# A decoder layer on one core: splitting the weights and forming the merged query weights inside the first sequence's work

## The chip, the core and the metric

The kernel runs on one core of a Trainium2 chip. The core has five engines that run their own instruction streams in order: PE (TensorE, matmuls, with its weight loads shown as PEld), DVE (VectorE), ACT (ScalarE), POOL (GpSimd) and SP (SyncE, which here only issues DMAs). They are tied together by semaphores alone. The metric is the device time of one execution in microseconds (us).

## What is computed

One pre-norm decoder layer on x of 2 x 1024 tokens with 512 channels: a windowed self-attention, a cross-attention to a context of 2 x 2048 tokens, and a feed-forward part. The reference, cut to what matters here:

```python
qkv = _layernorm(x) @ qkv_w.T + qkv_b            # 16 heads of 32; q and k scaled to length 1
attn = softmax(where(abs(i - j) <= 16 and (i - j) % 2 == 0, q @ k.T, -inf))
x = x + (attn @ v) @ out_w.T + out_b
q = _layernorm(x) @ Wq + bq
k, v = ctx @ Wk + bk, ctx @ Wv + bv
x = x + softmax(q @ k.T) @ v
x = x + (silu(x_n @ w_gate.T) * (x_n @ w_up.T)) @ w_down.T     # x_n = _layernorm(x), weights int / 127
```

The kernel never forms the cross-attention's keys. It multiplies the normalised x by one merged matrix, the product of Wq and Wk (`wp`), and the context itself is then the key. The biases go into a column `bqp`, a scalar `bqbk` and a row `wqb_row`; the value bias of the first attention goes through the output weights into `ob_row`.

## The kernel before

Every float32 matmul that matters is done as three matmuls on a high and a low part of each operand (`three`, L164 to L168: high x high, high x low, low x high). So each weight is split once: ACT casts the raw weight to the high part (`wqkv_h`), DVE subtracts it from the raw weight to get the low part (`wqkv_l`).

There are two blocks of engine programs in `attention_phase`. **The setup block** (L282 to L391) runs first and alone: SP loads all weights, POOL writes the constants (`ident`, `band`, `ones`, `hmask`, `mhalf`), ACT and DVE split Wq, Wk, the output weights and the first attention's weights `wqkv`, PE forms the bias rows and columns and the product `wp` in the four `score` banks, and ACT and DVE split that product. It ends with DVE copying the bias results. All engines meet at its end.

**The main block** (from L452) then goes through NS = 4 sequences `s` of 512 tokens in tiles of 128 tokens (ST = 4). For a sequence: DVE takes mean and variance of a tile (`spread1`), POOL the root (`root1`), ACT normalises (`norm1`), PE transposes (`transposes`), ACT and DVE split the result (`turned`), PE projects to queries and keys (`project_qk`) and to values (`project_v`). `p` is 0 or 1 for the first or second half of the head groups, and the columns of `wqkv` for p = 1 are not read before the loop. DVE copies q and k out with their bias (`qk_tile`), ACT squares, DVE sums (`square_sums`) and from the sums of four tiles finds 1 / length in a chain of 14 small instructions (`lengths`, L832 to L854), POOL scales q and k by it (`scale_units`, 128x1024 each), PE transposes them (`heads`, 8 transposes for a group), ACT and DVE split those (`heads_hi`, `heads_lo`). After that lead-in of sequence 0 a loop runs over `s` and n = 0 to 15, a unit being one of 4 head groups in one of 4 token tiles: `scores` on PE, `exp` on ACT, `mask` on POOL, `weighted` on PE. In each unit PE also does a piece of the next sequence's projections, or of the previous sequence's output and query projections. The later stages (cross-attention, feed-forward) follow.

The order on each engine is written out by hand in the code. PE's results other than scores go through `work`, a ring of four PSUM banks whose uses are listed in `ring_uses`; PE takes the n-th use only when the (n-4)-th has been read out (`take`, `wait_freed`). The use `("len", ...)` is one in which DVE computes the lengths inside the bank, so the fourth value tile of sequence 0 waits for the end of `lengths`. SP issues its DMAs in the order of its program, and waits in it hold back all that stands behind.

## Time and profile before

| what | value |
|---|---|
| median of 3 runs | 1280.5 us (1279.76 to 1282.55) |
| the profiled execution, its own time | 1279.2 us |
| its span in the profile | 1277.5 us |
| PE busy / DVE / ACT / POOL | 95% / 43% / 32% / 19% |
| setup block, up to the first instruction of the main block | 39.6 us |
| lead-in of sequence 0, up to the first projection of the loop | 39.6 to 75.0 us |

The span is what the trace covers; 1.7 us of the profiled execution lie around it. A busy share is taken over the whole span. PE's is high everywhere but at the start, so what is read for this change is the first 146 us, stretch by stretch. In a timeline row stand the start, the duration or the length of a merged stretch (x2, x16: so many instructions), the engine, the line, the operation with output and inputs, and in brackets the idle time before it and what ended that.

### The profile page before, as it was taken

Reading aid. Unit: us, or ns where it says so; the run is one execution under the profiler, and the core shown is the slowest. Engines: PE = TensorE matmul, PEld = TensorE weight load, DVE = VectorE, ACT = ScalarE, POOL = GpSimd, SP = SyncE. Lnnn points to the kernel's source line nnn. Section 1 sums busy time; section 2 is a strip of 40 time slices with the busy share of each in tenths; the row PEclk is TensorE's granted clock in tenths of the full one; section 3 lists DMA queues with packets and bytes.
Section 4 is the critical chain, followed back from the end, with each engine's and each line's share of the span. In section 5 each row is a group of like instructions: output and inputs, shape, how many; then the busy total and the mean of one; then the engine's idle time right before and its main releaser. Section 6 shows DMA issues by size and latency. Waiting matters only on the chain.

```text
span 1277.5 us, 16905 instructions
## 1 busy us (share of the span) xinstructions
PE 1219.5 (95%) x6760; PEld 984.0 (77%) x6760; DVE 553.8 (43%) x1030; ACT 414.7 (32%) x740; POOL 239.3 (19%) x230
## 2 busy tenths in 40 slices
PE   6889999999987989999999999999999999999998
PEld 4667777777755878888787888877888888888887
DVE  5446666585675643223554322334353123123212
ACT  4235454445353432322442222223332111111111
POOL 0136665655664110000000000000000000000000
PEclk9789999999979999999999999999999999999999
DMA  6200020200044341010250110043321001000000
GB/s 247 66 8 27 2 66 2 75 34 34 34 149 149 124 148 42 26 33 25 99 173 22 37 32 26 17 140 96 100 62 67 1 1 48 18 0 24 9 1 33
DMA packets 45763, 73.29 MB, mean 57 GB/s; under 512 B 4225, under 2 KB 16513, under 8 KB 45697
## 3 DMA queue, kind: packets, MB, share of 16 engines
q1 hardware_dynamic: 45696, 72.37, 17.3%
q8 instruction: 46, 0.75, 0.3%
q14 instruction: 21, 0.16, 0.0%
HBM read 55.58 MB, written 16.78 MB: 57 GB/s over the span
## 4 chain that ended last, share of the span: by engine, by line
PE 78%; DVE 6%; issue 5%; ACT 3%; POOL 3%; DMA 1%; DVEq 0%; POOLq 0%; ACTq 0%
PE work L166 13%; PE work L168 12%; PE work L167 12%; PE score L166 11%; PE score L168 11%; PE score L167 11%; PE score L1054 2%; PE work L1559 2%; DVE rsum L871 1%; PE score L1068 1%; PE work L1037 1%; PE work L1013 1%; POOL xs L556 1%; DVE ct_l L1439 1%; PE score L1072 1%
## 5 line engine op out<-in xcount | busy, mean ns | idle before, releaser
L166 PE MATMUL score<-fxt_h,w_hl 128*128 128x512 f32 x384 | 149.6, 390 | 0.8 <-DVE fxt_l L1822 0.8
L168 PE MATMUL score<-fxt_h,w_hl 128*128 128x512 f32 x384 | 149.4, 389 | 0.0
L167 PE MATMUL score<-fxt_l,w_hl 128*128 128x512 f32 x384 | 149.4, 389 | 0.0
L1842 DVE SCALAR_TENSOR_TENSOR hid<-score,gate 128x512 f32<-128x512 f32 x48 | 33.2, 691 | 236.6 <-ACT gate L1771 236.6
L1445 DVE TENSOR_TENSOR pt_l<-work,pt_h 128x512 fp32r<-128x512 f32 x64 | 44.0, 690 | 181.3 <-ACT pt_h L1372 181.3
L1771 ACT ACTIVATE gate<-score 128x512 f32<-128x512 f32 x48 | 28.7, 598 | 265.9 <-PE score L168 265.9
L166 PE MATMUL score<-ct_h,x_q_h 128*128 128x512 f32 x256 | 103.5, 404 | 3.9 <-DVE x_q_l L1434 3.2
L537 POOL TENSOR_TENSOR probs<-probs,band 128x544 f32<-128x544 f32 (+1 forms) x64 | 91.1, 1424 | 73.2 <-ACT probs L658 72.9
L166 PE MATMUL work<-cn,pt_h 128*128 128x512 f32 x256 | 101.6, 397 | 0.0
L168 PE MATMUL score<-ct_h,x_q_l 128*128 128x512 f32 x256 | 100.7, 393 | 0.0
L167 PE MATMUL score<-ct_l,x_q_h 128*128 128x512 f32 x256 | 100.2, 391 | 0.0
L168 PE MATMUL work<-cn,pt_l 128*128 128x512 f32 x256 | 99.9, 390 | 0.0
L167 PE MATMUL work<-cn,pt_h 128*128 128x512 f32 x256 | 99.7, 390 | 0.0
L166 PE MATMUL work<-wqkv_h,xt_h 128*128 128x512 f32 (+1 forms) x256 | 93.9, 367 | 2.3 <-DVE rnrm L854 1.9
L1372 ACT CAST pt_h<-work 128x512 fp32r<-128x512 f32 x64 | 37.2, 587 | 178.2 <-PE work L1559 178.2
L1351 POOL TENSOR_TENSOR xr<-xr,bv_row 128x512 f32<-128x512 f32 x16 | 21.5, 1342 | 392.3 <-DMA xr<-x_scratch 392.3
L168 PE MATMUL work<-wqkv_h,xt_l 128*128 128x512 f32 (+1 forms) x256 | 87.6, 342 | 0.0
L167 PE MATMUL work<-wqkv_l,xt_h 128*128 128x512 f32 (+1 forms) x256 | 87.5, 342 | 0.0
L166 PEld LDWEIGHTS score<-fxt_h,w_hl 128*128 128x128 f32 x384 | 72.1, 188 | 16.2 <-issue 1.2
L168 PEld LDWEIGHTS score<-fxt_h,w_hl 128*128 128x128 f32 x384 | 72.1, 188 | 15.1
L167 PEld LDWEIGHTS score<-fxt_l,w_hl 128*128 128x128 f32 x384 | 72.1, 188 | 14.8
L166 PE MATMUL work<-w_hl,hid_h 128*128 128x512 f32 x192 | 75.5, 393 | 0.9 <-DVE xr L1475 0.8
(180 smaller groups left out, 2474.3 us busy)
## 6 DMA issues: line engine op xcount, KB each, us to landing
x_stage<-in_ctx_t SPq DMA_DIRECT2D x16, 512.0 KB, 4.0
x_stage<-in_ctx_n SPq DMA_DIRECT2D x16, 512.0 KB, 4.1
x_in<-in_x SPq DMA_DIRECT2D x16, 256.0 KB, 2.7
xs<-in_x SPq DMA_DIRECT2D x4, 1024.0 KB, 5.4
x_scratch<-xs SPq DMA_DIRECT2D x4, 1024.0 KB, 4.4
qp_scratch<-xs SPq DMA_DIRECT2D x4, 1024.0 KB, 4.3
x_q_raw<-qp_scratch SPq DMA_DIRECT2D x16, 256.0 KB, 2.7
xr<-x_scratch SPq DMA_DIRECT2D x16, 256.0 KB, 2.7
```

Source lines behind the costliest of these rows:

```text
L166: pe.matmul(out, hi_s, hi_m, start=first, stop=False)
L167: pe.matmul(out, hi_s, lo_m, start=False, stop=False)
L168: return pe.matmul(out, lo_s, hi_m, start=False, stop=last)
L537: PL.tensor_tensor(probs[:, n % 2, :, 0:w], probs[:, n % 2, :, 0:w], band[:, c0:c0 + w].unsqueeze(1).to_broadcast([P, HPG, w]), ALU.mult). ...
L556: PL.tensor_tensor(xs[:, t, :], xs[:, t, :], ob_row[:], ALU.add).then_inc(xb_done, 1)
L1054: last = PE.matmul(out[a], kt[r, g % 2, c], qt[r, g % 2, :, lo:lo + w], start=first_mm, stop=last_mm)
L1351: nc.gpsimd.tensor_tensor(xr[:, par, :], xr[:, par, :], bv_row[:], ALU.add).then_inc(xb_done, 1)
L1372: nc.scalar.copy(pt_h[:, 4 * c:4 * c + 4, :], src.rearrange("p (k q) -> p k q", q=P)).then_inc(pth_done, 1)
L1445: V.tensor_tensor(pt_l[:, 4 * c:4 * c + 4, :], src.rearrange("p (k q) -> p k q", q=P), pt_h[:, 4 * c:4 * c + 4, :].bitcast(F32), ALU.subtr ...
L1559: last = PE.transpose(out[:, P * k:P * k + P], pr[:, 512 * c + P * k:512 * c + P * k + P], ident[:])
L1771: nc.scalar.activation(gate[:, f % 2, :], score[:, 2 * (f % 2), :], ACT.Silu, scale=WSCALE)\
L1842: V.scalar_tensor_tensor(hid[:], score[:, 2 * (f % 2) + 1, :], WSCALE, gate[:, f % 2, :], ALU.mult, ALU.mult).then_inc(hid_done, 1)
```

## The change

The setup block is gone. Its work stands in the programs of the main block, in the order of first use:

- SP issues the first three x tiles first, then the first half (p = 0) of `wqkv` in four pieces, then (after a wait on the first normalised tile, in `next_tile(3)`) a fourth x tile, the bias columns, Wq, Wk, the second half of `wqkv` in four pieces, and the output weights. The load of `xs` moves to the loop, behind the split of the output weights, whose raw copy now lies in the same memory.
- A list `parts` names all splits in order: four of p = 0 (128x768 each), `wide` (the key bias spread over 128 columns), Wq, Wk, four of p = 1, the second `wide`, the output weights. `part_hi(n)` is the cast on ACT, `part_lo(n)` the subtraction on DVE.
- PE: the bias row `wqb` (now 12 matmuls in split form, before 4 plain float32 ones) stands before the first value tile; `product(0)` and `product(1)` around the fourth value tile, `product(2)` and `product(3)` behind `heads`; the bias columns (20 matmuls of one column) behind the first `scores`; the row `ob` (12 matmuls) in unit n = 14 of sequence 0. The four uses `wqb`, `bq`, `bk` and `ob` go through the ring, which DVE empties.
- In the loop of sequence 0, ACT and DVE do one 128x512 split at n = 0 and the 128x2048 split of the output weights at n = 12.
- POOL writes the constants at the start of its main program.

```diff
+            if not s and n == 14:
+                yield ("ob",)
...
+            for t in range(3):
+                sp.dma_start(x_in[:, t, :], x_v[0][:, t, :]).then_inc(xin_landed[t], 16)
+            for k in range(DK):
+                sp.dma_start(raw[:, 0, k, :], wqkv_v[:, 0, k, :]).then_inc(wqkv_landed[0][k], 16)
...
+            def part_hi(n):
+                src, hi, _, landed, count = parts[n]
+                act.wait_ge(landed, count)
+                A.copy(hi, src).then_inc(set_hi, 1)
...
+            part_hi(KEYS)
+            part_hi(WQ)
             squares(0, 0, 2)
+            part_hi(WK)
             squares(0, 0, 3)
-            for t in range(ST):
+            for k in range(DK):
+                part_hi(SECOND + k)
+            for t in range(3):
                 v_tile(0, 0, t)
+            product_hi(0)
+            v_tile(0, 0, 3)
+            product_hi(1)
+            act.wait_ge(consts, CONSTS)
+            act.wait_ge(set_lo, VALUES)
             heads_hi(0, 0)
...
+                    if not s and n in (0, 12):
+                        part_hi(WO if n else VALUES)
...
+            def part_lo(n):
+                src, hi, lo, _, _ = parts[n]
+                dve.wait_ge(set_hi, n + 1)
+                V.tensor_tensor(lo, src, hi.bitcast(F32), ALU.subtract).then_inc(set_lo, 1)
...
             transposes("x", 0, 0)
             transposes("x", 0, 1)
+            pe.wait_ge(set_lo, DK)
             project_qk(0, 0, 0)
...
             project_qk(0, 0, 3)
+            pe.wait_ge(set_lo, WQ + 1)
+            bias_row(("wqb",), 0, q_h, q_l)
             leave(("len", 0, 0))
-            for t in range(ST):
+            for t in range(3):
                 project_v(0, 0, t)
+            pe.wait_ge(set_lo, WK + 1)
+            product(0)
+            project_v(0, 0, 3)
+            product(1)
             heads(0, 0)
             heads(0, 1)
+            product(2)
+            product(3)
+            pe.wait_ge(prod_lo, 2)
             scores(0, 0)
+            bias_columns()
+            pe.wait_ge(prod_lo, DK)
...
+                    if not s and n == 14:
+                        pe.wait_ge(set_lo, WO + 1)
+                        bias_row(("ob",), 1, wo_h, wo_l)
```

**DVE, lead-in of sequence 0**, from the second tile's sum of squares on. Before:

```order
L823 TENSOR_REDUCE ss<-sq 128x16
L817 TENSOR_TENSOR qk<-work,qkb_row 128x2x256
L823 TENSOR_REDUCE ss<-sq 128x16
L817 TENSOR_TENSOR qk<-work,qkb_row 128x2x256
L823 TENSOR_REDUCE ss<-sq 128x16
L832 TENSOR_SCALAR work<-ss 128x64
```

Between the sums of the second tile and the first instruction of `lengths` (L832) stand only the two remaining tiles. The same place after the change (line numbers of the changed kernel):

```order
L816 TENSOR_REDUCE ss<-sq 128x16
L902 COPY wide<-cols 128x1024
L805 TENSOR_TENSOR wide_l<-wide,wide_h 128x512
L805 TENSOR_TENSOR wq_l<-wq_raw,wq_h 128x2048
L810 TENSOR_TENSOR qk<-work,qkb_row 128x2x256
L816 TENSOR_REDUCE ss<-sq 128x16
L805 TENSOR_TENSOR wk_l<-wk_raw,wk_h 128x2048
L810 TENSOR_TENSOR qk<-work,qkb_row 128x2x256
L816 TENSOR_REDUCE ss<-sq 128x16
L911 COPY wqb_row<-work 128x512
L825 TENSOR_SCALAR work<-ss 128x64
```

Three subtractions and two copies have moved in ahead of `lengths`; four more subtractions (128x768) follow directly behind it.

**PE, from the last `heads` of the lead-in to the first projection of the loop.** Before:

```order
L1037 MATMUL work<-ident,qk 128x128 x16
L1054 MATMUL score<-qbd_h,kt_h 128x2x136 x2
L1054 MATMUL score<-qbd_l,kt_h 128x2x136 x2
L1054 MATMUL score<-qbd_h,kt_l 128x2x136 x2
L1054 MATMUL score<-qbd_h,kt_h 128x288 x2
L1054 MATMUL score<-qbd_l,kt_h 128x288 x2
L1054 MATMUL score<-qbd_h,kt_l 128x288 x2
L166 MATMUL work<-wqkv_h,xt_h 128x512
```

After, from the last three of the 24 matmuls of `product(2)` and `product(3)`, which stand behind the 16 transposes:

```order
L168 MATMUL score<-wk_h,wq_h 128x512
L169 MATMUL score<-wk_l,wq_h 128x512
L170 MATMUL score<-wk_h,wq_l 128x512
L1108 MATMUL score<-qbd_h,kt_h 128x2x136 x2
L1108 MATMUL score<-qbd_l,kt_h 128x2x136 x2
L1108 MATMUL score<-qbd_h,kt_l 128x2x136 x2
L1077 MATMUL work<-cols,wk_raw 128x1 x16
L1082 MATMUL work<-cols,wide 128x1 x4
L1108 MATMUL score<-qbd_h,kt_h 128x288 x2
L1108 MATMUL score<-qbd_l,kt_h 128x288 x2
L1108 MATMUL score<-qbd_h,kt_l 128x288 x2
L168 MATMUL work<-wqkv_h,xt_h 128x512
```

The products stand between the transposes and the first `scores`, the 20 one-column matmuls between the first and the second.

**DVE in units n = 12 to 14 of sequence 0**, from the end of `lengths` for sequence 1 on, after the change:

```order
L847 RECIPROCAL rnrm<-work 128x4x2x8
L864 RECIPROCAL rsum<-rsum 128x256
L805 TENSOR_TENSOR wo_l<-wo_raw,wo_h 128x2048
L864 RECIPROCAL rsum<-rsum 128x256
L853 TENSOR_TENSOR kt_l<-work,kt_h 128x512
L857 SCALAR_TENSOR_TENSOR qbd_l<-work,hmask,qbd_h 128x512 x2
L983 TENSOR_TENSOR ob_row<-work,ob_row 128x512
```

`wo_l` has come between the two halves of the softmax sum's reciprocal (`rsum`), which before followed each other at once; POOL's `out_scale`, and behind it `mask` and `scale_units`, wait for the second half.

## Rows read from the trace of the kernel before

**Rows 1.** The page: chain that ended last, and DMA issues (median us to landing).

```profile
PE 78%; DVE 6%; issue 5%; ACT 3%; POOL 3%; DMA 1%; DVEq 0%; POOLq 0%; ACTq 0%
...
x_in<-in_x SPq DMA_DIRECT2D x16, 256.0 KB, 2.7
```

**Rows 2.** Windows: stretch, length, busy by engine, PE clock, DMA share, GB/s.

```profile
0.00:39.60 39.60, 26.82 (x104) 17.98 (x104) 17.88 (x16) 14.63 (x12) 1.92 (x16) 0.96 0.56 199
39.60:74.97 35.37, 27.71 (x140) 22.77 (x140) 19.44 (x52) 13.30 (x23) 7.92 (x11) 0.80 0.19 60
...
146.00:1277.50 1131.50, 1097.48 (x5890) 891.42 (x5888) 473.14 (x875) 350.89 (x640) 187.20 (x168) 0.99 0.17 55
...
15.00:20.00 5.00, 5.00 (x17) 3.09 (x16) 2.55 (x2) 0.00 (x0) 0.00 (x0) 1.00 1.01 413
```

**Rows 3.** Timeline, the first weight cast, and the start of the main block.

```profile
6.10 1.90 ACT L331 CAST wq_h<-wq_raw 128x2048 fp32r<-128x2048 f32 x1 [4.01 <-DMA wq_raw<-in_wq_t]
...
39.63 0.69 DVE L790 BATCH_NORM_STATS2 stats<-x_in 128x6 f32<-128x512 f32 x1
...
41.80 0.81 ACT L609 ACTIVATE xn<-x_in,nb,rstd 128x512 f32<-128x512 f32 x1 [12.95 <-POOL nb L514]
...
45.18 0.80 PE L166 MATMUL work<-wqkv_h,xt_h 128*128 128x512 f32 x1 [0.39 <-DVE xt_l L811]
```

**Rows 4.** Timeline, from the last projection of the lead-in to the loop's first.

```profile
59.38 0.39 PE L168 MATMUL work<-wqkv_h,xt_l 128*128 128x512 f32 x1
...
61.99 0.23 DVE L832 TENSOR_SCALAR work<-ss 128x64 int32<-128x64 int32 x1
...
65.99 0.39 PE L166 MATMUL work<-wqkv_h,xt_h 128*128 128x256 f32 x1 [1.91 <-DVE rnrm L854]
66.02 3.79 POOL L531 TENSOR_TENSOR qk<-qk,rnrm 128x1024 f32<-128x1024 f32 x2 [18.21 <-DVE rnrm L854]
...
67.99 3.46 PE L1037 MATMUL work<-ident,qk 128*128 128x128 f32 x16 [0.27 <-POOL qk L531]
...
74.98 0.80 PE L166 MATMUL work<-wqkv_h,xt_h 128*128 128x512 f32 x1
```

**Rows 5.** Groups by line of the setup: busy us, mean ns | idle before.

```profile
L351 DVE TENSOR_TENSOR wqkv_l<-w_raw,wqkv_h 128x1536 fp32r<-128x1536 f32 x4 | 6.8, 1752 | 4.4 <-ACT wqkv_h L336 4.4
...
L348 DVE TENSOR_TENSOR wq_l<-wq_raw,wq_h 128x2048 fp32r<-128x2048 f32 x1 | 2.3, 2287 | 0.0
...
L344 DVE COPY wide<-cols 128x1024 f32<-128x1024 f32 x1 | 0.7, 695 | 10.3 <-DMA cols<-in_qkv_b 10.3
...
L336 ACT CAST wqkv_h<-w_raw 128x1536 fp32r<-128x1536 f32 x4 | 5.6, 1476 | 5.6 <-DMA w_raw<-in_wqkv_t 5.6
```

**Rows 6.** Timeline of PE in the setup: products, one-column matmuls, output bias row.

```profile
16.77 0.79 PE L166 MATMUL score<-wk_h,wq_h 128*128 128x512 f32 x1
...
28.06 0.95 PE L381 MATMUL work<-cols,wide 128*128 128x1 f32 x8
...
32.44 4.52 PE L389 MATMUL work<-wo_raw,wide 128*128 128x512 f32 x6
```

**Rows 7.** Windows in which PE's granted clock (third value from the end) is halved.

```profile
33.40:36.60 3.20, 3.20 (x5) 1.32 (x4) 0.00 (x0) 0.00 (x0) 0.00 (x0) 0.50 0.00 0
67.76:70.95 3.19, 2.96 (x13) 2.66 (x14) 0.69 (x1) 1.91 (x4) 2.05 (x2) 0.50 0.02 5
```

**Rows 8.** Timeline of units n = 12 to 14 of sequence 0.

```profile
129.26 0.65 ACT L658 ACTIVATE probs<-score 128x576 f32<-128x576 f32 x1 [0.83 <-PE score L1054]
...
133.40 1.09 PE L1037 MATMUL work<-ident,qk 128*128 128x128 f32 x8 [1.36 <-POOL qk L531]
...
139.20 1.09 PE L1037 MATMUL work<-ident,qk 128*128 128x128 f32 x8 [0.46 <-POOL qk L531]
```

**Rows 9.** Timeline of sequence 1, unit n = 8: POOL and DVE side by side.

```profile
192.37 1.43 POOL L537 TENSOR_TENSOR probs<-probs,band 128x576 f32<-128x576 f32 x1
192.61 1.74 DVE L884 SCALAR_TENSOR_TENSOR xn<-xn,wqb_row 128x512 f32<-128x512 f32 x1
```

More of the change, by code:

```diff
@@ L258, in attention_phase @@
     x_v = x.rearrange("(s t p) d -> s p t d", t=ST, p=P)
[L260 to L263 removed]
+    raw = over.put("w_raw", [P, 2, DK, PW])
+    raw_o = over_xs.put("wo_raw", [P, DK, D])
+    raw_q = over_wo.put("wq_raw", [P, DK, D])
+    raw_k = over_wo.put("wk_raw", [P, DK, D])
     q_h = over_ot.put("wq_h", [P, DK, D], F32R)
     q_l = over_ot.put("wq_l", [P, DK, D], F32R)
[L266 to L267 removed]
+    wide = over_sums.put("wide", [P, 2, DK, P])
+    wide_at = over_x2t.at
     k_h = over_x2t.put("wk_h", [P, DK, D], F32R)
     k_l = over_x2t.put("wk_l", [P, DK, D], F32R)
[L270 to L271 removed]
+    over_k = Plan(nc, wide_at)
+    wide_h = [over_rows.put("wide0_h", [P, DK, P], F32R)]
+    wide_l = [over_rows.put("wide0_l", [P, DK, P], F32R)]
+    wide_h.append(over_k.put("wide1_h", [P, DK, P], F32R))
+    wide_l.append(over_k.put("wide1_l", [P, DK, P], F32R))
+    wqkv_landed = [[sem(f"wqkv_landed{p}{k}") for k in range(DK)] for p in range(2)]
+    w_landed = [sem(f"w_landed{n}") for n in "qko"]
+    cols_landed = sem("cols_landed")
+    qkb_landed = sem("qkb_landed")
+    ob_landed = sem("ob_landed")
     set_hi = sem("set_hi")
@@ new lines, in attention_phase @@
+    wqkv_v = wqkv_t.rearrange("(k p) (g n) -> p g k n", p=P, g=2)
+    pieces_of = [[(raw[:, p, k, :], wqkv_h[:, k, p, :], wqkv_l[:, k, p, :], wqkv_landed[p][k], 16)
+                  for k in range(DK)] for p in range(2)]
+    bias_of = [(wide[:, n], wide_h[n][:], wide_l[n][:], wide_ready, 1) for n in range(2)]
+    parts = pieces_of[0] + [bias_of[0], (raw_q[:], q_h[:], q_l[:], w_landed[0], 16),
+                            (raw_k[:], k_h[:], k_l[:], w_landed[1], 16)]
+    parts += pieces_of[1] + [bias_of[1], (raw_o[:], wo_h[:], wo_l[:], w_landed[2], 16)]
@@ L473, in _ @@
                     next_tile(k)
+                if not s:
+                    sp.wait_ge(set_lo, WO + 1)
+                    sp.dma_start(xs[:], x_v[0]).then_inc(xs_landed, 16)
                 if s:
@@ L903, in _ @@
             square_sums(0, 0, 1)
+            dve.wait_ge(cols_landed, 64)
+            V.tensor_copy(wide[:], cols[:, 1:3, :].unsqueeze(3).to_broadcast([P, 2, DK, P])).then_inc(wide_ready, 1)
+            part_lo(KEYS)
+            part_lo(WQ)
             qk_tile(0, 0, 2)
             square_sums(0, 0, 2)
+            part_lo(WK)
             qk_tile(0, 0, 3)
             square_sums(0, 0, 3)
+            wait_filled(dve, ("wqb",))
+            V.tensor_copy(wqb_row[:], bank(("wqb",))).then_inc(dve_freed, 1)
             lengths(0, 0)
+            for k in range(DK):
+                part_lo(SECOND + k)
+            product_lo(0)
+            product_lo(1)
+            dve.wait_ge(consts, CONSTS)
             heads_lo(0, 0)
+            product_lo(2)
+            product_lo(3)
             for s in range(NS):
@@ L959, in _ @@
                         spread2(s - 1, n - 5)
+                    if not s and n == 0:
+                        part_lo(VALUES)
+                    if not s and n == 12:
+                        part_lo(WO)
+                    if not s and n == 14:
+                        wait_filled(dve, ("ob",))
+                        dve.wait_ge(ob_landed, 16)
+                        V.tensor_tensor(ob_row[:], bank(("ob",)), ob_row[:], ALU.add).then_inc(dve_freed, 1)
             s = NS - 1
@@ L1038, in heads, with product, bias_columns, bias_row @@
                     last.then_inc(filled, 1)
+            def product(m):
+                for e in range(DK):
+                    last = three(PE, score[:, m, :], q_h[:, e, P * m:P * m + P], q_l[:, e, P * m:P * m + P],
+                                 k_h[:, e, :], k_l[:, e, :], e == 0, e == DK - 1)
+                last.then_inc(prod_ready, 1)
+            def bias_columns():
+                out = take(("bq",))
+                pe.wait_ge(wide_ready, 1)
+                for m in range(DK):
+                    for e in range(DK):
+                        last = PE.matmul(out[:, m:m + 1], raw_k[:, e, P * m:P * m + P], cols[:, 0, e:e + 1],
+                                         start=e == 0, stop=e == DK - 1)
+                last.then_inc(filled, 1)
+                out = take(("bk",))
+                for e in range(DK):
+                    last = PE.matmul(out[:, 0:1], wide[:, 0, e, :], cols[:, 0, e:e + 1],
+                                     start=e == 0, stop=e == DK - 1)
+                last.then_inc(filled, 1)
+            def bias_row(key, n, w_h, w_l):
+                out = take(key)
+                for e in range(DK):
+                    last = three(PE, out, wide_h[n][:, e, :], wide_l[n][:, e, :], w_h[:, e, :], w_l[:, e, :],
+                                 e == 0, e == DK - 1)
+                last.then_inc(filled, 1)
             def scores(s, n):
@@ L1138, in _ @@
                             project_query(s - 1, m)
+                    if not s and n == 14:
+                        pe.wait_ge(set_lo, WO + 1)
+                        bias_row(("ob",), 1, wo_h, wo_l)
                     if n == 7:
```

199 lines of the change are left out of this document (75 added, 124 removed).

## The prediction

> **What bounds the kernel now.** I read the page's chain first: PE holds 78% of the path that ends last [rows 1]. The windows then say where it does not [rows 2]. From 146 us on PE is busy for 1097.5 of 1131.5 us (97%), so whatever is won before that point is simply handed on to the end. The first 39.6 us are the setup block, in which x is not touched, and of the 35.4 us of lead-in behind it PE is busy for 27.7, partly at a mean clock of 0.80. The timeline shows the seam: statistics of the first x tile start at 39.63 and the first projection at 45.18 [rows 3]. So the question is how early the loop's first projection, at 74.98 us [rows 4], can start once the two stretches are one, and what the loop pays for the work pushed into it.
>
> **Step 1, the first projection.** One x tile takes 2.7 us from issue to landing [rows 1]; Wq, issued first before, was used at 6.10 after an issue at about 0.8 [rows 3]. I put the first x tile at 3.8. From statistics to normalisation it is 41.80 - 39.63 = 2.2 us [rows 3], so ACT normalises from 6.0 on. ACT then does two normalisations (1.6), two casts, one `turned` (0.6) and two casts; a cast of 768 columns is half of 1.476 = 0.74 [rows 5]. DVE, from 8.6 on, does four subtractions of half of 1.752 = 0.88 and one `turned` (0.7): 8.6 + 4.2 = 12.8. The data are there: three x tiles and four pieces are 2.36 MB, at 413 GB/s [rows 2] 5.7 us behind a first 2.1 (2.7 less the tile's own 0.6) and an issue at 0.8, so 8.6 us, where the last piece is cast at about 10.5. First projection at 13.1 in place of 45.18: 32.1 us earlier.
>
> **Step 2, up to the last projection of the lead-in.** Nothing new stands there; 59.38 + 0.23 - 45.18 = 14.4 us are copied [rows 3, 4], the half-clock matmuls at its start included. It ends at 27.5. Nothing of Wq and Wk is late: Wq is issued at about 11.3, behind the wait on the first normalised tile and four slow column loads, and needs some 5.3 us, against a cast that cannot start before 26.3.
>
> **Step 3, DVE becomes the bound.** The sums of the second tile end at about 24.9 (this place shifted by 32.1). Behind them DVE and ACT work hand in hand and nothing of it overlaps: copy `wide` 0.7 [rows 5], cast of `wide` 0.6, cast of Wq 1.90 [rows 3], its subtraction 2.29 [rows 5]: 30.4. PE has waited since 27.5, 3 us, for `set_lo`. Third tile and its square 1.4, cast of Wk 1.9, subtraction 2.3: 36.0. Then tile, square and sum as before (from 59.8 to 61.99, 2.2 us), the copy of `wqb` 0.7 and `lengths` (61.99 to 65.95, 4.0) [rows 4]: 42.9. PE meanwhile does `wqb` (12 matmuls at 0.235, 2.8), three value tiles and `product(0)`, and waits in three places for this chain.
>
> **Step 4, PE is the bound again.** From 42.9: the fourth value tile 1.7 (65.99 to 67.7) [rows 4]; `product(1)` 2.8, a quarter of 28.06 - 16.77 = 11.3 [rows 6]; two `heads` at full clock 2 x 1.09 = 2.2 [rows 8], where they took 3.46 before [rows 4]; `product(2)` and `(3)` 5.6; first `scores` 0.7; one-column matmuls 32.44 - 28.06 = 4.4 [rows 6]; second `scores` 0.8. Sum 18.2: the loop's first projection at 61.1. The one-column matmuls hide the wait for the first `exp`, and `product(1)` hides POOL's scaling (1.9 for each of two [rows 4]).
>
> **Step 5, the clock.** In the trace the granted clock fell to 0.50 (1.2 GHz) for some 3 us after the one-column matmuls, and again after PE's wait of 1.9 us before the fourth value tile [rows 4, 7]. In the new order there are waits of about 3, 2 and 1 us. A halved 3.2 us costs 1.6 us of dense work. Those that fall before 42.9 are hidden under DVE's chain; I charge 1.0 for one that reaches beyond it, between 0 and 3.2. The fall behind the one-column matmuls takes the place of one that the old order had at the loop's start and is charged at nothing.
>
> **Step 6, DVE against POOL.** In sequence 1 a DVE instruction of 512 columns with two SBUF inputs, started inside a POOL instruction, took 1.74 us [rows 9], where one of 2048 columns without POOL beside it takes 2.29 [rows 5]; it ended 0.55 after POOL's. So such a subtraction and a POOL instruction run one after the other. The four subtractions of the second half start at 42.9 together with POOL's two scalings: 3.5 + 3.8 us in series. If they alternate, the second scaling ends at 48.6 and costs the second `heads` 0.25 us; if DVE goes first with all four, 2.1 us. I take 0.25, since in the row the one that came second waited for one instruction only. The Trainium skill ("SBUF — State Buffer", section "SBUF: two separate sides") speaks of an exclusive lock on a port pair that VectorE with two SBUF inputs and GpSimd share, held for the whole instruction. The trace agrees, with the 1.74 us above. If nothing were shared, steps 6 and 7 would come out some 0.6 us better.
>
> **Step 7, the loop of sequence 0.** At n = 12 the cast of the output weights (1.9) stands ahead of an `exp` that started at 129.26 [rows 8], about 0.8 after ACT was free. It slips by 1.1, with it `mask`, the first scaling and the `heads` at 133.40, where PE waits for POOL already. DVE's 2.29 comes before the second reciprocal, so `out_scale`, the next `mask` and the second scaling slip by about 3.8 in all, and the `heads` at 139.20, which waits for POOL too. PE's own 12 matmuls (2.8) lie within these 3.8, not on top. So 3.8; bounds 2.8 (PE's work alone) and 5.5 (all three in a row for the most part). At n = 0 two short splits and two small copies: 0.3, hidden but for hops.
>
> **The sum.** 74.98 - 61.1 = 13.9; less 1.0, 0.25, 3.8 and 0.3 is 8.5 us. The span goes from 1277.5 to 1269.0 and, with the 1.7 us around it, the profiled execution from 1279.2 to 1270.7. The median of the three runs stood 1.3 above that execution, so I predict 1280.5 - 8.5 = **1272.0 us**. By its own range this case covers 1269 to 1275: the clock term 0 to 3.2, step 7 2.8 to 5.5, and about 1 us either way on when x lands.
>
> **Rivals.**
> - *The hand-offs cost more.* DVE keeps ahead of POOL at 42.9 (another 1.9), the clock is halved twice in step 4 (another 2.2), step 7 takes 5.5 (another 1.7): gain 2.7 to 4, time near 1277. For it: from 25 to 43 us every step is cast, then subtraction, then tile, with no slack at all. Against: each of these waits frees PE's next one.
> - *Less than the sum.* If the wait of `heads` for POOL at n = 13 to 15 absorbs the 3.8 down to PE's 2.8, no halved clock reaches beyond 42.9, and x lands a microsecond sooner, the gain is 8.5 + 1.0 + 1.0 + 1.0 + 0.5 for waits in the first units that the shift closes: 12, time near 1268.5.
> - *It doesn't bring the work forward.* The order of SP's queue holds the data back: Wq and Wk stand behind a wait and behind four loads of 4-byte elements. Each microsecond by which Wq misses 26.3 moves everything. It would have to land at 35 in place of 17 for nothing to be won. The same would follow if the setup's cost came back as idle PE in the chain of step 3. Time 1280.5.
> - *Slower: the clock stays at half.* PE now starts in bits, with waits between, and ends the lead-in on one-column matmuls. If it stays at 1.2 GHz from 13 to 61 us, the 108 matmuls of 512 columns pay 0.2 each (21.6), the value tiles 5.4, transposes 1.8, the one-column ones up to 4.4. Less 3.6 already counted and 7 hidden in DVE's chain this is 22.6, and the time is 1280.5 - 8.5 + 22.6 = 1294.6. It decides from 8.5 us on, about 43 matmuls of 512 columns at half speed off DVE's chain. For it: the lead-in's mean clock is 0.80 today [rows 2]. Against: every fall in it lasted about 3 us once matmuls were dense again [rows 7].
>
> **Chances.** Forecast 0.64, hand-offs 0.16, better 0.10, not brought forward 0.06, slower by the clock 0.04. The range of 8 in 10 reaches from 1267.5 to 1277.5: below lies a part of the better case, above the last two and a part of the first rival. A difference of 0.2% (2.6 us) is about what a measurement of this kernel can tell from none. Faster by more: 0.64 + 0.10 + nearly all of 0.16, so 0.89. Within: 0.07. Slower: 0.04.
>
> **What would show it.** Step 1: first matmul on `wqkv_h` at 13 us. Step 3: a wait of PE for DVE of about 3 us before the row `wqb`, and `lengths` ending near 43. Step 4: the loop's first projection at 62 to 63. Step 5: windows at clock 0.50 behind those waits. Step 6: subtractions of 768 columns that take well over 0.9 us beside POOL's scaling. Step 7: sequence 1 starting 8 to 9 us earlier than before, but the loop's unit 12 some 12 us earlier. Wrong would be the prediction above all if PE's clock or the arrival of x differ, since both act on everything behind them.

## The result, and the profile after

The changed kernel takes **1268.1 us** (median of 4 runs, 1267.3 to 1268.8) beside 1281.5 us for the kernel before in the same comparison (4 runs, 1279.8 to 1282.9). The ratio is 0.9896, 95% interval 0.9878 to 0.9913. The profiled execution took 1268.8 us with a span of 1267.0; before it was 1279.2 and 1277.5, so the two traces differ by 10.5 us. The forecast was 1272.0 with a range of 1267.5 to 1277.5 and a gain of 8.5 us. Direction, mechanism and range held; the gain was put too small, and the median lies just below the 1269 to 1275 that the forecast case allowed itself.

PE's share of the chain that ended last stays about where it was (78% in [rows 1]), since everything behind the start still hangs on PE:

```profile
PE 79%; DVE 7%; issue 5%; ACT 3%; POOL 3%; DMA 2%; SPq 0%; DVEq 0%; POOLq 0%; ACTq 0%
```

Windows of the changed kernel, to be laid beside [rows 2]; the columns are stretch, length, busy us of PE, PE's weight loads, DVE, ACT and POOL (instructions), granted PE clock, DMA share, GB/s:

```profile
0.00:12.96 12.96, 1.97 (x8) 1.43 (x8) 7.28 (x21) 7.60 (x10) 4.40 (x22) 1.00 0.85 261
12.96:60.05 47.09, 44.08 (x232) 37.31 (x232) 31.56 (x51) 18.87 (x29) 7.24 (x5) 0.93 0.32 118
60.05:128.12 68.07, 63.92 (x576) 49.26 (x575) 44.11 (x86) 33.78 (x60) 37.80 (x33) 0.97 0.11 32
```

The first ends at the first projection, the second at the loop's first projection, the third at the second `heads` of the second sequence, the row that stood at 139.20 before [rows 8]. PE is now busy for 44.1 of the 47.1 us of lead-in. The record of the clock begins only at about 16 us; what lies before it is shown as 1.00. The same third stretch in the kernel before:

```profile
74.98:139.20 64.22, 60.65 (x565) 46.80 (x563) 39.77 (x83) 31.62 (x58) 38.33 (x34) 0.98 0.07 18
```

So 14.9 us are won up to the loop's first projection (74.98 to 60.05), and 3.85 us are given back within the loop (64.22 to 68.07). That leaves 11.1 at the second `heads`, and 10.5 at the end of the span. Up to the loop's first projection PE's idle time fell from 20.4 to 14.0 us and its busy time from 54.5 to 46.1: the row `ob` has left this stretch for the loop, and less of it runs at half clock. In the loop PE's busy time rose by 3.3 us (60.65 to 63.92) and its idle time by 0.6.

The start, timeline of the changed kernel (start, duration, engine, line, operation; in brackets the idle time before it and its releaser):

```profile
3.68 0.69 DVE L773 BATCH_NORM_STATS2 stats<-x_in 128x6 f32<-128x512 f32 x1 [3.68 <-issue]
...
12.96 0.79 PE L168 MATMUL work<-wqkv_h,xt_h 128*128 128x512 f32 x1 [4.14 <-DVE wqkv_l L805]
```

These answer to 39.63 and 45.18 in [rows 3]. The 12 projections of the first tile, in the kernel before and after, and the first seven of the latter by themselves:

```profile
45.18:50.46 5.28, 5.28 (x12) 4.07 (x13) 1.61 (x6) 1.22 (x2) 0.82 (x2) 0.50 0.45 126
...
12.96:17.22 4.26, 4.26 (x12) 3.37 (x13) 1.50 (x6) 0.81 (x1) 0.82 (x2) 1.00 0.90 327
12.96:15.70 2.74, 2.74 (x7) 2.16 (x8) 1.50 (x6) 0.13 (x1) 0.82 (x2) 1.00 0.91 337
```

The 1.00 of the last two is the missing record. Up to 15.69 these matmuls start 0.43 us apart, the pace at clock 0.50 in the kernel before, and from there 0.23 us apart, the pace at 1.00. The next rows are the hand-offs between ACT and DVE that split the merged weights, with PE's wait for them:

```profile
23.70 0.68 DVE L902 COPY wide<-cols 128x1024 f32<-128x1024 f32 x1
...
24.94 1.90 ACT L563 CAST wq_h<-wq_raw 128x2048 fp32r<-128x2048 f32 x1
...
26.88 2.29 DVE L805 TENSOR_TENSOR wq_l<-wq_raw,wq_h 128x2048 fp32r<-128x2048 f32 x1 [1.12 <-ACT wq_h L563]
...
29.22 0.50 PE L168 MATMUL work<-wq_h,wide_h 128*128 128x512 f32 x1 [2.72 <-DVE wq_l L805]
...
32.26 2.29 DVE L805 TENSOR_TENSOR wk_l<-wk_raw,wk_h 128x2048 fp32r<-128x2048 f32 x1 [1.11 <-ACT wk_h L563]
...
40.42 0.56 DVE L847 RECIPROCAL rnrm<-work 128x64 f32<-128x64 f32 x1
```

Copy, cast, subtraction and matmul follow one another without overlap: 23.70, 24.94, 26.88, 29.22. DVE idles 1.1 us for each cast, and PE 2.7 us for the subtraction. `lengths` ends at 40.42 + 0.56 = 40.98. Behind that point, to be read beside [rows 4]:

```profile
40.90 6.94 DVE L805 TENSOR_TENSOR wqkv_l<-w_raw,wqkv_h 128x768 fp32r<-128x768 f32 x4
41.07 5.09 POOL L486 TENSOR_TENSOR qk<-qk,rnrm 128x1024 f32<-128x1024 f32 x2 [25.53 <-DVE rnrm L847]
...
45.65 1.91 PE L1061 MATMUL work<-ident,qk 128*128 128x128 f32 x16
...
53.51 3.89 PE L1077 MATMUL work<-cols,wk_raw 128*128 128x1 f32 x32
...
57.26 1.84 PE L1082 MATMUL work<-cols,wide 128*128 128x1 f32 x8
...
60.05 0.79 PE L168 MATMUL work<-wqkv_h,xt_h 128*128 128x512 f32 x1
```

The 16 transposes run in one piece, without a wait, at full clock; before they took 3.46 us. The one-column matmuls (each is recorded twice here, so 16 and 4) last from 53.51 to 59.04. Two windows show where the granted clock fell, which answers to [rows 7] (third value from the end):

```profile
29.90:33.40 3.50, 3.50 (x10) 2.76 (x9) 1.83 (x2) 2.32 (x2) 0.00 (x0) 0.55 0.02 5
57.30:64.10 6.80, 6.80 (x25) 5.69 (x26) 0.32 (x2) 0.65 (x1) 1.42 (x1) 0.52 0.00 0
```

The first lies behind PE's wait of 2.7 us. The second begins under the one-column matmuls and lasts 6.8 us (57.0 to 63.8 in the record of the clock), twice what [rows 7] had led me to expect; the next section shows that this differs from execution to execution. Last, the loop of sequence 0 where the output weights are split, to be read beside [rows 8]:

```profile
113.88 1.91 ACT L563 CAST wo_h<-wo_raw 128x2048 fp32r<-128x2048 f32 x1
...
115.69 0.65 ACT L623 ACTIVATE probs<-score 128x576 f32<-128x576 f32 x1
...
118.44 3.41 DVE L805 TENSOR_TENSOR wo_l<-wo_raw,wo_h 128x2048 fp32r<-128x2048 f32 x1
...
119.76 1.09 PE L1061 MATMUL work<-ident,qk 128*128 128x128 f32 x8 [2.17 <-POOL qk L486]
...
123.59 1.29 POOL L501 TENSOR_TENSOR o_sc<-o_sc,rsum 128x512 f32<-128x512 f32 x1 [3.89 <-DVE rsum L864]
...
128.12 1.09 PE L1061 MATMUL work<-ident,qk 128*128 128x128 f32 x8 [0.26 <-POOL qk L486]
```

The first `heads` came 13.6 us earlier than before (133.40), the second 11.1 (139.20). The row of POOL is `out_scale`, which waits for DVE's second reciprocal behind `wo_l`. Before, it waited 1.3 us there:

```profile
134.66 1.29 POOL L546 TENSOR_TENSOR o_sc<-o_sc,rsum 128x512 f32<-128x512 f32 x1 [1.31 <-DVE rsum L871]
```

### The profile page after: what moved, and what is told of

Same layout as the page of the kernel before. It is cut to its first block, busy times and chain, and to the rows that moved or that the text cites. A ratio compares the mean times of both kernels' runs of the same rounds, so it can differ in the third digit from the quotient of the medians.

```text
span 1267.0 us, 16936 instructions
## 1 busy us (share of the span) xinstructions
PE 1212.9 (96%) x6768; PEld 984.0 (78%) x6768; DVE 561.9 (44%) x1036; ACT 415.6 (33%) x746; POOL 240.5 (19%) x230
## 4 chain that ended last, share of the span: by engine, by line
PE 79%; DVE 7%; issue 5%; ACT 3%; POOL 3%; DMA 2%; SPq 0%; DVEq 0%; POOLq 0%; ACTq 0%
PE work L168 13%; PE work L170 12%; PE work L169 12%; PE score L168 11%; PE score L170 11%; PE score L169 11%; PE score L1108 2%; PE work L1629 2%; DVE rsum L864 1%; PE score L1122 1%; PE work L1061 1%; POOL xs L511 1%; DVE ct_l L1509 1%; PE score L1126 1%; PE work L1037 1%
```

## The experiments

Every kernel here is the changed kernel with the edit shown. The figure to compare with is that of the first one, 1268.6 us. The kernel before, run on the same chips, had medians of 1279.8 us (first four experiments) and 1278.6 us (the other four, on another chip). The changed kernel itself was not run beside the last four. Laid against the kernel before instead, their standing beside the changed kernel comes out 1.1 us worse than the differences of medians given below, so differences of 1 to 2 us there rest on the traces and not on the times.

### The changed kernel again

No edit.

> The changed kernel once more, beside the kernel before, for a second profile of it and a closer ratio. The forecast was 8.5 us of gain, the two profiled executions differ by 10.4 and the medians by 13.5. If the sum's terms are what acts, the profile shows again the loop's first projection near 60 us and a span near 1267. If the further 3 us between profiles and medians are real and lie in the kernel, they show as fewer stretches at half clock in one of the two; if they are the scatter of the kernel before, the ratio moves towards 0.991 to 0.992.

**Measured:** 1268.6 us (1267.8 to 1270.6, 6 runs) beside 1279.8 (13 runs); ratio 0.9913 (0.9894 to 0.9933), so 11.1 us. That is what the expectation named for scatter of the kernel before. Its trace has the loop's first projection at 59.65 and the second `heads` at 127.62, half a microsecond before the first trace's. The window of the loop:

```profile
59.65:127.62 67.97, 63.82 (x576) 49.19 (x575) 44.12 (x86) 33.76 (x60) 37.82 (x33) 0.97 0.11 32
```

In the 13 runs of the kernel before, the slower a run is, the lower by and large its mean granted clock:

| kernel before, single runs | time, us | mean granted clock |
|---|---|---|
| fastest | 1277.4 | 0.981 |
| median | 1279.8 | 0.979 |
| slowest | 1285.5 | 0.976 |

The kernels' single runs can therefore differ by some microseconds with the same program. The gain is best taken from this comparison with its many runs: 11.1 us, and 10.4 between the profiled executions of 1279.2 and 1268.8.

Where in the lead-in the clock is at half also differs from execution to execution. The fourth, sixth and seventh experiments below leave the lead-in's order of work as it is, so there are five traces of it (us; the half-clock stretches from the record of the clock):

| trace | 12 matmuls of the first tile | end of `lengths` | at half clock | one-column matmuls | loop's first projection |
|---|---|---|---|---|---|
| changed kernel, first | 4.26 | 40.98 | 29.6 to 33.1, 57.0 to 63.8 | 5.53 | 60.05 |
| changed kernel, again | 4.18 | 40.50 | 29.1 to 32.5, 56.4 to 63.2 | 5.59 | 59.65 |
| fourth experiment | 4.40 | 41.14 | 30.0 to 33.4, 57.3 to 64.1 | 5.38 | 60.10 |
| sixth experiment | 5.28 | 42.00 | 59.5 to 63.0 | 4.56 | 59.75 |
| seventh experiment | 5.29 | 41.58 | 59.0 to 62.4 | 4.55 | 59.43 |

In the last two all 12 matmuls of the first tile go at the slow pace, as before the change, and what follows is later by 1 us or so. But the fall behind PE's wait for `wq_l` is missing, and the one-column matmuls run at full clock, with a fall of 3.4 us behind them:

```profile
54.11:58.66 4.55, 4.55 (x42) 4.54 (x40) 2.77 (x5) 0.73 (x2) 1.33 (x1) 1.00 0.01 4
58.90:62.50 3.60, 3.60 (x13) 2.71 (x12) 0.03 (x1) 0.65 (x1) 1.42 (x1) 0.53 0.00 0
```

The loop's first projection comes at the same time in both kinds. The 1.6 us that `wqb` is faster at full clock come back as a wait for DVE's chain (timeline of the sixth experiment):

```profile
36.22 0.39 PE L168 MATMUL work<-wqkv_h,xt_h 128*128 128x256 f32 x1 [1.55 <-DVE qk L810]
```

Why an execution takes the one course or the other, no run here tells.

### The first two products behind the heads

```diff
-            pe.wait_ge(set_lo, WK + 1)
-            product(0)
             project_v(0, 0, 3)
-            product(1)
             heads(0, 0)
             heads(0, 1)
+            pe.wait_ge(set_lo, WK + 1)
+            product(0)
+            product(1)
             product(2)
```

ACT and DVE read them out at the corresponding place.

> One part of the change undone: the products 0 and 1 no longer stand around the fourth value tile, all four stand behind the transposes of q and k. Theory (they cover PE's wait for the end of lengths, 38.7 to 41.4 us, and for POOL's two scalings, 41.1 to 46.2): the two waits come back, 2.3 us before the fourth value tile and 3 us before and within the transposes, so the loop's first projection moves from 60.0 to about 64.5 and the kernel is 4 to 5 us slower than the change. Rival (only the early start of x matters, PE is the bound anyway): under 1 us.

**Measured:** 1275.0 us (8 runs), ratio to before 0.9957 (0.9939 to 0.9975): 6.4 us slower than the changed kernel. The loop's first projection stands at 66.44. PE's timeline, three rows with their waits:

```profile
36.25 0.39 PE L168 MATMUL work<-wqkv_h,xt_h 128*128 128x256 f32 x1 [1.50 <-DVE qk L810]
...
42.08 0.39 PE L168 MATMUL work<-wqkv_h,xt_h 128*128 128x256 f32 x1 [2.15 <-DVE rnrm L847]
...
47.24 1.09 PE L1061 MATMUL work<-ident,qk 128*128 128x128 f32 x8 [0.85 <-POOL qk L486]
```

The first is not the edit's: it stands in the sixth and seventh traces too (1.55, 1.54), where the products are in their places, and like them this trace has the slow start (`lengths` ends at 42.03) and no fall at `wqb`. The second is a wait of the kernel before (1.91 for `rnrm` in [rows 4]). `product(0)` and `product(1)`, 2.8 us each, fill this time in the changed kernel, where PE waits 0.3 us in all from `wqb` to the loop. The like-for-like stretch is from the end of `lengths` to the loop's first projection: 24.4 us here, and 17.8 in the sixth and seventh traces. `product(0)`, 2.8 us, has moved into it, the wait of 0.85 is new, and behind the wait of 2.15 the clock falls from 42.6 to 46.0, so that the fourth value tile takes 2.3 us in place of 1.4 and the first `heads` 1.73 in place of 1.09. The one-column matmuls take 5.6 us in place of 4.6. So the place of these 24 matmuls is worth the 6 us or so, more than the 4 to 5 expected: somewhat more than half of it in the wait and in work that no longer fills one, the rest in the clock.

### The splits of Wq and Wk earlier

ACT casts the spread bias before the fourth normalisation, Wq behind the third tile's split and Wk behind the fourth's, all ahead of the squares of the last two tiles. DVE copies and splits `wide` before the first tile of queries and keys, and Wk directly behind Wq:

```diff
             spread1(0, 3)
+            dve.wait_ge(cols_landed, 64)
+            V.tensor_copy(wide[:], ...)
+            part_lo(KEYS)
...
             square_sums(0, 0, 1)
-            dve.wait_ge(cols_landed, 64)
-            V.tensor_copy(wide[:], ...)
-            part_lo(KEYS)
             part_lo(WQ)
+            part_lo(WK)
             qk_tile(0, 0, 2)
-            square_sums(0, 0, 2)
-            part_lo(WK)
             qk_tile(0, 0, 3)
+            square_sums(0, 0, 2)
             square_sums(0, 0, 3)
```

> The splits of the key bias, Wq and Wk are moved ahead: casts into ACT's idle time between 12.7 and 24.4 us, the copy of the key bias ahead of the first q and k tile on DVE, the subtractions of Wq and Wk directly behind the second sum, without waiting for casts. Theory (DVE's chain of casts and subtractions is the bound from 26.5 to 41 us, step 3): PE's wait of 2.7 us before the row wqb goes, with it the halved clock at 31 to 34 us (1.6 us) and two waits of 0.3: first projection of the loop at 55.5 to 56, 4 us faster than the change. Rival (PE's own work is the bound): only the 2.7 us wait goes or less, since later waits grow, 0 to 2 us. Second rival (the loads of Wq and Wk are not there yet): no change, ACT waits for a DMA.

**Measured:** 1265.7 us, ratio 0.9886 (0.9866 to 0.9906), 2.9 us better than the changed kernel, where 4 had been expected. DVE's timeline:

```profile
24.63 2.28 DVE L805 TENSOR_TENSOR wq_l<-wq_raw,wq_h 128x2048 fp32r<-128x2048 f32 x1
...
26.83 2.29 DVE L805 TENSOR_TENSOR wk_l<-wk_raw,wk_h 128x2048 fp32r<-128x2048 f32 x1
...
36.44 0.56 DVE L847 RECIPROCAL rnrm<-work 128x64 f32<-128x64 f32 x1
```

The two subtractions follow one another with no wait for a cast, PE's wait of 2.7 us is gone, and `lengths` ends at 37.0 in place of 40.98. So the chain of hand-offs did bound the changed kernel up to here; without it PE is the bound, with 43.7 of the 43.8 us of lead-in busy. The loop's first projection came only 3.0 us earlier than in the run above (56.64), not the 4: this execution had the slow start of 5.3 us for the first tile, the halved clock now lay under the end of the lead-in, and the one-column matmuls took 6.1 us.

```profile
50.40:57.20 6.80, 6.80 (x41) 6.44 (x41) 2.21 (x5) 0.46 (x1) 1.27 (x1) 0.64 0.01 2
```

The profiled executions differ by 0.8 us only (1267.0 and 1267.8). That of this kernel is among the slower of its six runs (1264.3 to 1267.8).

### The output weights' split earlier, as one piece

```diff
-                    if not s and n in (0, 12):
+                    if not s and n in (0, 10):
                         part_hi(WO if n else VALUES)
...
-                    if not s and n == 12:
+                    if not s and n == 10:
                         part_lo(WO)
...
-            if not s and n == 14:
+            if not s and n == 13:
                 yield ("ob",)
```

> The split of the output weights moves from n = 12 to n = 10, the row ob from n = 14 to n = 13, ahead of the transposes for which PE waits for POOL (2.17 us in the changed kernel). Theory (step 7: at n = 12 to 14 the cast delays exp, the subtraction delays the second reciprocal and is in POOL's way): POOL's scalings come back by 1 and 2.5 us, the 12 matmuls fall into PE's wait, 2.5 to 3 us faster than the change. Rival (PE's 12 matmuls cost their 2.8 us wherever they stand): under 0.5 us.

**Measured:** 1268.0 us (1263.9 to 1268.9), ratio 0.9900 (0.9879 to 0.9922): 0.6 us, not to be told from none. The stretch up to the second `heads` shrank by 0.8 us (67.97 to 67.16), where 2.5 to 3 had been expected. A miss. Timeline of units 10 to 13:

```profile
110.56 2.29 DVE L805 TENSOR_TENSOR wo_l<-wo_raw,wo_h 128x2048 fp32r<-128x2048 f32 x1 [1.64 <-ACT wo_h L563]
111.12 2.94 POOL L492 TENSOR_TENSOR probs<-probs,band 128x544 f32<-128x544 f32 x1 [1.03 <-ACT probs L623]
...
113.49 0.63 ACT L602 ACTIVATE sq<-qk 128x512 f32<-128x512 f32 x1 [2.44 <-DVE qk L810]
...
115.22 0.44 PE L1122 MATMUL score<-probs,v 128*32 128x136 f32 x8 [1.46 <-ACT o_sc L632]
...
121.99 1.09 PE L1061 MATMUL work<-ident,qk 128*128 128x128 f32 x8
```

The wait for POOL before the first `heads` is gone, but a new one stands earlier. This time the mask was the one that started second: 2.94 us, where such a mask takes 1.43 on the mean. But the new wait comes another way. DVE copies the tile of queries and keys (`qk`, at 112.77) only when the subtraction is over, ACT waits 2.44 us for it before it squares, and only then reads the previous result (`o_sc`) out of its bank, for which PE waits 1.46 us. At both places tried, a 2.29 us subtraction puts off what stands behind it on DVE, and the instruction of POOL's that it meets.

### Most one-column matmuls left out

`product`, `heads` and `scores` stay; of the 20 one-column matmuls for the bias columns two are left, so `bqp` and `bqbk` are not what they should be. DVE copies the one column in place of four.

```diff
-                for m in range(DK):
-                    for e in range(DK):
-                        last = PE.matmul(out[:, m:m + 1], raw_k[:, e, P * m:P * m + P], cols[:, 0, e:e + 1], ...)
+                last = PE.matmul(out[:, 0:1], raw_k[:, 0, 0:P], cols[:, 0, 0:1], start=True, stop=True)
```

The four of the second kind are cut to one likewise.

> In the changed kernel 18 of the 20 one-column matmuls are left out (2 remain, so that the ring is filled; the bias column of the query and its scalar are then not the reference's). They take 53.5 to 59.0 us there, 5.5 us, and the granted clock is halved from 57.3 to 64.1. Theory A (these matmuls are what brings the clock down): the loop's first projection moves from 59.7 to 54.0 or earlier, less about 1 us of wait for the first exp, the halved stretch from 57.3 on is gone or short, and the kernel is 5.5 to 6.5 us faster than the change. Theory B (the clock falls anyway, for the value tiles and waits before them): the halved stretch stays, 3.5 to 4.5 us faster.

**Measured:** 1262.9 us, ratio 0.9875 (0.9848 to 0.9902): 5.7 us better than the changed kernel (4.6 by the ratios to the kernel before). Two rows of PE's timeline and the window from there:

```profile
54.77 0.40 PE L1103 MATMUL score<-qbd_h,kt_h 64*128 64x288 f32 x2 [0.29 <-DVE wp_l L799]
...
55.37 0.50 PE L168 MATMUL work<-wqkv_h,xt_h 128*128 128x512 f32 x1
```

```profile
45.00:55.37 10.37, 10.07 (x63) 8.18 (x61) 8.42 (x11) 5.66 (x10) 2.18 (x2) 1.00 0.00 0
55.37:62.00 6.63, 6.63 (x47) 5.10 (x46) 3.37 (x7) 2.35 (x4) 3.21 (x3) 1.00 0.01 2
```

The granted clock stays at 1.00 in both windows, where the changed kernel has 0.52 from 57.3 to 64.1. In the other eight traces of changed kernels, which all have the 20 matmuls, it falls under or just behind them. Of the 5.9 us at the second `heads` (127.62 to 121.68) 4.3 are won by the loop's first projection and 1.7 behind it. The first is the matmuls' own time, a part of it at half clock. The second goes with the clock they leave behind: 3.6 us of the loop are at half clock in the trace above and none here, which by an estimate from the pace (half of it) is 1.8 us. Hardly anything waited for these matmuls to be over: only 0.29 us came back as a wait.

### Most matmuls of the row `ob` left out

Nine of the 12 matmuls go, so the row is not complete.

```diff
-                for e in range(DK):
+                for e in range(DK if n == 0 else 1):
```

> In the changed kernel 9 of the 12 matmuls of the row ob at n = 14 are left out (3 remain; the output bias is then not the reference's). The split of the output weights stays at n = 12. Theory (step 7: the chain DVE, POOL sets when the transposes for sequence 1's second group start, PE's matmuls lie within it): these transposes start less than 0.5 us earlier than the 127.6 to 128.1 us of the change, and the kernel is at most 0.5 us faster. Rival, favoured by the fourth experiment (PE's own work is the price): 2 us earlier and 2 us faster.

**Measured:** 1269.6 us, ratio 0.9922 (0.9899 to 0.9946), 1.0 us above the changed kernel and thus no gain. With nine matmuls less the second `heads` stands where it stood (127.53 beside 127.62):

```profile
127.53 1.75 PE L1061 MATMUL work<-ident,qk 128*128 128x128 f32 x8 [1.74 <-POOL qk L486]
```

The wait for POOL there has grown from 0.27 to 1.74 us, and one of 0.5 for `kt_l` has come: together the 2.1 us of the nine matmuls. As long as the split stands there in one piece, PE's 12 matmuls only fill a wait for POOL's chain, which the split puts off.

### The output weights' split in four pieces

```diff
-    parts += pieces_of[1] + [bias_of[1], (raw_o[:], wo_h[:], wo_l[:], w_landed[2], 16)]
+    parts += pieces_of[1] + [bias_of[1]]
+    parts += [(raw_o[:, k, :], wo_h[:, k, :], wo_l[:, k, :], w_landed[2], 16) for k in range(DK)]
...
-                    if not s and n in (0, 12):
-                        part_hi(WO if n else VALUES)
+                    if not s and n in (0, 8, 9, 10, 11):
+                        part_hi(WO + n - 8 if n else VALUES)
...
-                    if not s and n == 12:
-                        part_lo(WO)
+                    if not s and 8 <= n < 12:
+                        part_lo(WO + n - 8)
```

The row `ob` stands in unit 13 as in the fourth experiment.

> As the fourth experiment, but the split of the output weights goes in four pieces of 128x512 at n = 8 to 11 in place of one of 128x2048 at n = 10, where mask took 2.94 us beside it and PE waited 1.5 us for ACT's copy at n = 12. Theory (the one long piece made that new wait): PE's waits in the loop of sequence 0 fall from 3.3 us to under 1.5, from the loop's first projection to the transposes of sequence 1's second group it takes 65.5 us in place of 67.2, and the kernel is 2 to 2.5 us faster than the change. Rival (PE has no more to win there than its 12 matmuls leave): no more than 0.7 us faster than the change.

**Measured:** 1266.0 us, ratio 0.9893 (0.9871 to 0.9916), 2.6 us better than the changed kernel (1.5 by the ratios to the kernel before).

```profile
59.43:124.87 65.44, 63.55 (x576) 49.09 (x575) 45.65 (x89) 33.56 (x62) 39.40 (x33) 0.98 0.10 33
```

65.44 us in place of 67.97, and PE waits 1.9 us in the whole stretch, where it waited 4.2. The loop's start is at half clock for 3.0 us here and 3.6 there, so about 0.3 of the 2.5 us are the clock's (an estimate at half the pace). Against the fourth experiment, with 4.0 us at half clock, 1.2 of 1.7 us are left. One piece takes DVE 0.68 us alone, and one that meets a mask 1.67, but POOL is never put off by more than one piece. Of the two places tried and the two grains, the grain mattered more; the pieces also stand in other units (8 to 11) than the one piece did. What is left over the kernel before, 1.2 us (65.44 beside 64.22), is now PE's work: its busy time is 2.9 us longer and its waits 1.7 shorter.

### Both: early splits and four pieces

> The early splits of the third experiment (3 us) and the pieces of the seventh together. If the two places are independent: 3 + 2 = 5 us faster than the change, near 1263.5 us. If the seventh brings nothing, near 1265.5 us as the third.

**Measured:** **1262.6 us** (1261.2 to 1265.1, 4 runs), ratio 0.9871 (0.9847 to 0.9896), the best kernel of the study: 6.0 us below the changed one and 16.0 below the kernel before (4.9 below the changed one by the ratios).

```profile
56.57:121.95 65.38, 63.45 (x577) 49.00 (x575) 45.65 (x89) 33.53 (x62) 39.41 (x33) 0.98 0.11 33
```

The loop's first projection stands at 56.57 as with the early splits, and the stretch behind it is as long as with the four pieces. The two gains (2.9 and 2.6) add up within the noise: they lie in separate stretches of PE's path.

## Why the prediction was right, and where its sizes were off

The reading of the profile held: PE bounds all but the start, and what is won there reaches the end of the span but for 0.6 of 11.1 us. Of the rivals, the one named "less than the sum" came nearest (12 us, 1268.5), though of its terms only one came: no halved clock reached from DVE's chain beyond the end of `lengths`. POOL's wait absorbed nothing, and x landed no sooner. The argument against the slowest rival, that every fall of the clock in the old lead-in lasted about 3 us once matmuls were dense, was a misreading: the window 45.18 to 50.46 shows 5.3 us of dense matmuls at 0.50. Step by step (the measured column is the first trace):

| step | forecast | measured |
|---|---|---|
| 1: first projection | 13.1 | 12.96 |
| 2: lead-in's last projection ends | 27.5 | 26.5 |
| 3: PE's wait before `wqb` | 3 | 2.7 |
| 3: end of `lengths` | 42.9 | 40.98 |
| 4 and 5: from there to the loop's first projection, with POOL's 0.25 | 19.45 | 19.07 |
| 4: one-column matmuls | 4.4 | 5.5 |
| 6: wait of the second `heads` | 0.25 | none |
| 7: loop of sequence 0 | 3.8 + 0.3 | 3.85 |
| gain at the loop's first projection, clock and POOL charged | 12.6 | 14.9 |

- **Step 1** was right to 0.15 us, from durations in the setup's rows and one landing time.
- **Step 2** copied 14.4 us from the kernel before, "the half-clock matmuls at its start included". The new stretch had less of them: the first tile's query and key projections took 4.26 us, from 12.96 to 17.22, and 5.28 before. That is the 1.0, and it belongs to the execution: in the sixth and seventh traces they took 5.28 and 5.29, as copied.
- **Step 3**, the chain of hand-offs, took 17.2 us from the second tile's sums (23.78 to 40.98); the forecast had 18.0, from 24.9 to 42.9. The experiment with earlier splits shows that it is the bound: without the hand-offs `lengths` ends 4.0 us sooner, and 5.0 against the sixth trace, which has the slow start too.
- **Steps 4 and 5** came out right in sum, 0.4 off, but for reasons that cancel, and that is luck. The clock did not fall between 33.4 and 57.0; where it was at half before that, the chain of DVE hid it: `wqb` took 4.4 us in place of 2.8 at no cost, and in the traces without this fall the time came back as a wait. That frees the charge of 1.0. The 16 transposes took 1.7 us from start to next start and not 2.2: the 1.09 of [rows 8] includes the end of the last one, over which the next matmul already runs. Against that, PE came to the fourth value tile 0.5 us late, because `product(0)` was not done. The step that failed is the sentence that the fall behind the one-column matmuls "is charged at nothing". In three traces of the five they took 5.4 to 5.6 us in place of 4.4 and the clock was at half for 6.8 us; the loop's part of it was 3.6 to 4.0 us, beside 2.8 in the kernel before. In the other two the forecast's 4.4 and 3.2 came nearly true (4.6 and 3.4). Without most of them the kernel is 5.7 us faster (4.6 by the ratios).
- **Step 6** had the mechanism. The four subtractions and the two scalings stretched each other to 6.94 and 5.09 us, in turns as assumed, but `product(1)` still hid it, and PE went through `heads` without a wait. That the two hold each other up came in as forecast, and cost nothing at this place.
- **Step 7** was right in size, and in cause as far as the subtraction goes; the sum is luck in part. The first `heads` slipped by 1.3 us against the loop's first projection (14.9 less 13.6; forecast 1.1) and the second by 3.85. Counted from the loop's first projection, `lengths` of sequence 1 ends 0.5 us later than before (56.87, 56.38), which is what 0.9 us more at half clock come to at half the pace; the step had no such term here. The second reciprocal ends 3.9 us later (63.46, 59.60), and POOL's `out_scale` waits for nothing else (3.89 us). So the slip of the second `heads` is this 0.5 and the subtraction: `wo_l` takes 3.41 us beside POOL, 1.1 more than the 2.29 that the step counted. The 1.1 us by which the cast puts off `exp`, which the step added, is not in this chain. The two errors cancel. With the row's matmuls left out the time stays; with the split in pieces 2.5 us of it are gone.

So the forecast was 2.3 us short at the loop's first projection (1.1 from steps 1 and 2, 0.8 from step 3, 0.4 from steps 4 to 6), and the loop's 0.25 us go the same way. At the end of the span 0.6 of that are lost again. This explains the two profiled executions, 10.4 apart. The medians are 11.1 to 13.5 apart. The forecast put the median 1.3 above the profiled execution; single runs of the kernel before lie between 1277.4 and 1285.5 and follow the granted clock, so the rest of the 13.5 is in the sampling of few runs. **Open** stays why the clock's mean differs from run to run of one program. The time at half clock, summed over a trace from about 16 us on, was 51.5 us before, 38.0 and 37.5 in two traces of the changed kernel, and 51 with the early splits, whose runs are faster nevertheless. In the traces before, after (first) and with the early splits the lowest stretch of 100 us is the same, from 350 to 450 us, far behind anything that was edited: mean clock 0.88 before, 0.90 after, 0.87 with the early splits. No run here tells what sets its length.

## What to carry to other kernels

When a setup block is folded into the first stage, the work moves onto chains of hand-offs: read which engine waits for the other's half of a split, and put the halves one instruction apart, before anyone needs them. A long instruction of a helping engine inside a tight loop costs by its grain: as four pieces of 0.7 us the split cost PE 2.5 us less than as one of 2.3 (about 2.2 with the clock taken out), and moving the one piece saved 0.8. Taking away the matmuls that filled the wait, in its place, saved nothing. And small work that PE does at the end of a dense stretch is to be priced with the clock it leaves behind, and that price differs between executions of one program: 5.5 or 4.6 us for the matmuls themselves and 6.8 or 3.4 us at half clock.

## What was not expected of the hardware

- **DVE and POOL hinder each other in both directions.** A subtraction with two SBUF inputs of 128x2048 takes 2.29 us alone and 3.41 beside POOL; one of 128x768 about 0.9 alone and 2.67 beside POOL's scaling. POOL's mask took 2.94 us when it started 0.56 us into a 2.29 us subtraction, and its two scalings 5.09 beside four subtractions, 3.79 without [rows 4]. When both had a row of such work, in the lead-in, they took turns. This is the case that the forecast took; the other was that DVE goes first with all four. The Trainium skill ("SBUF — State Buffer", section "SBUF: two separate sides") has a VectorE instruction with two SBUF inputs and a GpSimd instruction that reads SBUF lock a shared port pair, whichever starts first, for the whole instruction. The rows here agree: the subtraction that started at 41.71, inside the scaling of 41.07 to 43.57, ended at 44.38, 0.8 us behind it.

```profile
41.07 2.50 POOL L486 TENSOR_TENSOR qk<-qk,rnrm 128x1024 f32<-128x1024 f32 x1 [25.53 <-DVE rnrm L847]
41.71 2.67 DVE L805 TENSOR_TENSOR wqkv_l<-w_raw,wqkv_h 128x768 fp32r<-128x768 f32 x1
```

- **One-column matmuls.** PE is busy all the time in the 5.5 us that they take, and still the granted clock goes to half (0.52) under them and stays there for 6.8 us, most of it in dense work that follows. In two traces of five it goes to half only behind them, for 3.4 us, and they take 4.6 us. With two of them left it stays at 1.00.
